# A selective scan between two ternary FFNs: a ring of five states in place of four, and the product with C written over the state

## The reference, cut to what matters

```python
skip = resid_norm @ W_skip                      # D=512 -> E=1024
x = _silu(conv(resid_norm @ W_in) + conv_b)     # 4 taps
delta = softplus(x @ W_delta_1 @ W_delta_2 + b_delta_2)
Bm, Cm = x @ W_B, x @ W_C                       # N=16 states
...
def step(h, inp):
    A_bar = jnp.exp(d_l[:, :, None] * A)
    h = h * A_bar + (d_l * x_l)[:, :, None] * B_l[:, None, :]
    y_l = jnp.einsum('ben,bn->be', h, C_l)
...
y_skip = (y + x * W_D) * _silu(skip)
return resid + y_skip @ W_out
```

## Time and profile before

| what | value |
|---|---|
| three runs, us | 2936.71, 2939.00, 2941.12; median 2939.0 |
| the profiled execution | 2940.29 us, its span 2938.7 |
| mean granted clock of PE | 0.97 |
| busy, share of the span | PE 90%, DVE 86%, POOL 82%, ACT 65% |
| chain that ended last | PE 61%, POOL 12%, DVE 8%, ACT 5%, issue 5%, DMA 3% |

### The profile page before, as it was taken

The page is one execution under the profiler, slowest core; times in us unless marked ns, Lnnn a source line. Parts: engine busy times, 40 slices in busy tenths (PEclk is TensorE's granted clock), DMA queues, the critical chain, the costliest instruction groups (busy, mean ns, idle before and its releaser), DMA issues.

```text
span 2938.7 us, 51656 instructions
## 1 busy us (share of the span) xinstructions
PE 2657.0 (90%) x17527; PEld 2054.0 (70%) x17527; DVE 2534.3 (86%) x3233; ACT 1900.3 (65%) x4428; POOL 2412.7 (82%) x2179
## 2 busy tenths in 40 slices
PE   4776899999999999999999999999999999999778
PEld 4555677776867777686777768677777867777555
DVE  6377899898889999898988989899998989899892
ACT  6375767666676766667676666767666676766651
POOL 1178888888898898989888898998989898897991
PEclk9888899999999999999999999999999999999898
DMA  7022222222222212222222131222213222221320
GB/s 261 31 60 69 62 53 69 49 53 72 51 70 53 70 46 55 73 51 69 53 65 50 48 80 44 71 58 64 51 49 79 48 69 57 65 51 48 87 55 15
DMA packets 91260, 185.22 MB, mean 63 GB/s; under 512 B 12220, under 2 KB 30456, under 8 KB 90488
## 3 DMA queue, kind: packets, MB, share of 16 engines
q1 hardware_dynamic: 72280, 113.76, 12.1%
q0 software_dynamic: 18720, 68.17, 11.8%
HBM read 104.82 MB, written 8.91 MB: 39 GB/s over the span
## 4 chain that ended last, share of the span: by engine, by line
PE 61%; POOL 12%; DVE 8%; ACT 5%; issue 5%; DMA 3%; POOLq 0%; DVEq 0%; ACTq 0%
PE ps L1560 20%; PE ps L1571 14%; PE ps L1583 10%; PE ps L1522 8%; POOL h L743 6%; PE ps L1632 5%; DVE h L1294 4%; DMA xw<-hc 3%; POOL hc L757 2%; PE ps L1593 2%; ACT ps L990 2%; DVE xc L1367 1%; POOL u L850 1%; POOL hl L842 1%; PE ps L1613 1%
## 5 line engine op out<-in xcount | busy, mean ns | idle before, releaser
L743 POOL TENSOR_TENSOR h<-u,bb 128x1024 f32<-128x1024 f32 x512 | 1247.1, 2436 | 82.5 <-PE ps L1522 36.7
L990 ACT ACTIVATE ps<-delta,a_neg 128x255 f32<-128x255 f32 x2048 | 877.0, 470 | 537.8 <-DVE h L1294 536.3
L1294 DVE TENSOR_TENSOR_SCAN h<-ps,h 128x512 f32<-128x512 f32 x1024 | 1189.5, 1203 | 27.3 <-ACT ps L990 13.2
L1560 PE MATMUL ps<-xh,q_up 128*128 128x256 f16 x2048 | 466.7, 275 | 38.0 <-DVE xl L1233 29.7
L1560 PE MATMUL ps<-xh,q_gate 128*128 128x256 f16 x2048 | 466.1, 274 | 28.4 <-DVE xw L1400 28.4
L1323 DVE SCALAR_TENSOR_TENSOR y<-ps,ccur,y 128x512 f32<-128x512 f32 x700 | 487.6, 737 | 1.7 <-PE ps L1522 1.1
L1522 PE MATMUL ps<-ident,h 128*128 128x128 f32 x3056 | 413.7, 278 | 64.0 <-DVE y L1323 58.8
L1560 PE MATMUL ps<-xl,q_up 128*128 128x256 f16 x2048 | 466.6, 275 | 0.0
L1560 PE MATMUL ps<-xl,q_gate 128*128 128x256 f16 x2048 | 465.5, 274 | 0.0
L1522 PEld LDWEIGHTS ps<-ident,h 128*128 128x128 f32 x3056 | 353.8, 142 | 135.4 <-issue 59.0
L842 POOL TENSOR_TENSOR hl<-act,hh 128x512 f16<-128x512 f32 x256 | 314.1, 1231 | 148.7 <-ACT hh L1015 148.7
(11 more groups left out here) (137 smaller groups left out, 3827.5 us busy)
## 6 DMA issues: line engine op xcount, KB each, us to landing
xw<-hc POOLq DMA_DIRECT2D x130, 512.0 KB, 4.5
bb<-b_scratch SPq DMA_DIRECT2D x224, 256.0 KB, 3.1
cplane<-c_scratch SPq DMA_DIRECT2D x130, 128.0 KB, 3.1
xs<-in_L_attn_resid_dram SPq DMA_DIRECT2D x17, 512.0 KB, 3.7
out_dram<-xs SPq DMA_DIRECT2D x16, 512.0 KB, 4.2
wraw<-in_L_ffn_W_up_dram SPq DMA_DIRECT2D x4, 1024.0 KB, 9.6
wraw<-in_L_ffn_W_gate_dram SPq DMA_DIRECT2D x4, 1024.0 KB, 12.5
wraw<-in_L_ffn_W_down_dram SPq DMA_DIRECT2D x4, 1024.0 KB, 14.1
```

The source lines that it names most:

```text
L743: pl.tensor_tensor(h[:, s % RING, :, :], u[:, :, :], bb[:, planes_of(s) % 2, s % PLANES:s % PLANES + 1, :].broadcast_to([P, HE, CH]), ALU. ...
L990: ins = ac.activation(abar[r][:, e, 1:], delta[:, k, 1:], ACT.Exp, scale=a_neg[:, k, n:n + 1])
L1294: v.tensor_tensor_scan(hr, abar[r].rearrange("p e t -> p (e t)"), hr, 0.0, ALU.mult, ALU.add).then_inc(scanned, 1)
L1560: ins = te.matmul(pp[:, f * CH:(f + 1) * CH], w[:, d, col:col + P], part[:, d, :], start=(d == 0 and part is xh), stop=(d == DB - 1 and pa ...
```

## The change

The ring has five slots, numbered by the running step (S % 5) in place of s % 4; `hc` is gone, so the memory is the same. The product with C is written over the state in its slot. It therefore waits for `carry_saved` of its own state, and the transfer reads the slot. The wait for the transfer before moves from ahead of the product to between product and transfer. A slot that held a product is free when its transfer has landed (`elem_added`), no more when the product is done. Every `u_times_b` waits for its planes of B, where before only the first of a pair did. `hidden_low` waits for the one before it. Three lists would move work from POOL to DVE (`UB_ON_DVE`, `Z_ON_DVE`, `LOW_ON_DVE`); they are empty, so the code for it issues nothing, and SP gets a second semaphore entry ahead of a load.

```diff
-RING = 4
+RING = 5
 ACTS = 2
+UB_ON_DVE = []
+Z_ON_DVE = []
+LOW_ON_DVE = {1: [], 2: []}
...
-        hc = sb("hc", [P, HE, CH])
...
-                    sp.wait_ge(ub_ready, STEPS * (c - (q < 2)) + last + 1)
+                    need(sp, ub_ready, ub_before(c - (q < 2), last + 1, False))
+                    sp.sem_inc(sp_go, 1)
+                    need(sp, dve_ub_ready, ub_before(c - (q < 2), last + 1, True))
                     sp.sem_inc(sp_go, 1)
...
-                if s == 0 or q > planes_of(s - 1):
-                    need(pool, bb_loaded[q % 2], 16 * planes_loaded(i, q))
...
+                if s in UB_ON_DVE:
+                    return
+                need(pool, bb_loaded[q % 2], 16 * planes_loaded(i, q))
                 used = S - RING
...
                 elif S >= RING:
-                    need(pool, times_c, elems_before(used // STEPS, used % STEPS) + 1)
+                    need(pool, elem_added, 16 * (elems_before(used // STEPS, used % STEPS) + 1))
...
                 need(pool, scanned, 2 * S + 2)
+                need(pool, carry_saved, S + 1)
+                go()
+                hs = h[:, S % RING, :, :]
+                pl.tensor_tensor(hs, hs, cplane[:, k:k + 1, :].broadcast_to([P, HE, CH]), ALU.mult).then_inc(times_c, 1)
+                need(pool, xw_ready, 2 * i + half + 1)
                 need(pool, elem_added, 16 * g)
-                go()
-                pl.tensor_tensor(hc[:, :, :], h[:, s % RING, :, :], cplane[:, k:k + 1, :].broadcast_to([P, HE, CH]),
-                                 ALU.mult).then_inc(times_c, 1)
-                need(pool, xw_ready, 2 * i + half + 1)
                 need(pool, times_c, g + 1)
-                pool.dma_start(xw[:, half * HE:(half + 1) * HE, :], hc[:, :, :], accum_op=ALU.add).then_inc(elem_added, 16)
+                pool.dma_start(xw[:, half * HE:(half + 1) * HE, :], hs, accum_op=ALU.add).then_inc(elem_added, 16)
...
                 need(pool, hh_ready, g + 1)
+                need(pool, hl_ready, g)
```

More of the change, by code:

```diff
@@ L317, in elems_before, with ub_before @@
     return sum(whole) + sum(k < s for k in elem_of(c))
+def ub_before(c, s, on_dve):
+    mine = [k for k in range(STEPS) if (k in UB_ON_DVE) == on_dve]
+    return len(mine) * c + sum(k < s for k in mine)
 def rows_before(c, s):
@@ L884, in run @@
                     for q in range(QT):
-                        if after(ph, f"YT_{q}", 0, s):
+                        if after(ph, f"YT_{q}", 0, s) and q not in Z_ON_DVE:
                             gated(ph, i, q)
                     for kind, p in hidden_units(ph, s):
-                        hidden_low(ph, i, kind, p)
+                        if p not in LOW_ON_DVE[kind]:
+                            hidden_low(ph, i, kind, p)
                     if after(ph, "DN1_1", 0, s):
@@ L995, in save_carry @@
                 need(sc, scanned, 2 * (STEPS * i + s + 1))
-                ac.activation(carry[:, s // N, :, state_of(s)], h[:, s % RING, :, CH - 1], ACT.Copy).then_inc(carry_saved, 1)
+                ac.activation(carry[:, s // N, :, state_of(s)], h[:, (STEPS * i + s) % RING, :, CH - 1], ACT.Copy).then_inc(carry_saved, 1)
             def first_decay(c, half):
@@ L1285, in _, with u_times_b @@
             ve.wait_ge(scale_step, 12)
+            def u_times_b(i, s):
+                S, half, n = STEPS * i + s, s // N, state_of(s)
+                q, g = planes_of(s), ub_before(i, s, True)
+                need(ve, bb_loaded[q % 2], 16 * planes_loaded(i, q))
+                need(ve, u_ready, 2 * i + half + 1)
+                need(ve, x0_ready, 2 * i + half + 1)
+                used = S - RING
+                if S >= RING and not is_elem(used // STEPS, used % STEPS):
+                    need(ve, hT_ready, 2 * rows_before(used // STEPS, used % STEPS) + 2)
+                elif S >= RING:
+                    need(ve, elem_added, 16 * (elems_before(used // STEPS, used % STEPS) + 1))
+                need(ve, carry_saved, used + 1)
+                go()
+                v.tensor_tensor(h[:, (STEPS * i + s) % RING, :, :], u[:, :, :],
+                                bb[:, q % 2, s % PLANES:s % PLANES + 1, :].broadcast_to([P, HE, CH]),
+                                ALU.mult).then_inc(dve_ub_step, 1)
+                need(ve, dve_ub_step, g + 1)
+                v.tensor_tensor(h[:, (STEPS * i + s) % RING, :, 0], h[:, (STEPS * i + s) % RING, :, 0], a0[:, half, :, n], ALU.add).then_inc(dve_ub_ready, 1)
             def scan_of(i, s):
                 S = STEPS * i + s
-                need(ve, ub_ready, S + 1)
+                if s in UB_ON_DVE:
+                    need(ve, dve_ub_ready, ub_before(i, s + 1, True))
+                else:
+                    need(ve, ub_ready, ub_before(i, s + 1, False))
                 for r in range(2):
                     need(ve, abar_ready, 2 * S + r + 1)
-                    hr = h[:, s % RING, 2 * r:2 * r + 2, :].rearrange("p e t -> p (e t)")
+                    hr = h[:, (STEPS * i + s) % RING, 2 * r:2 * r + 2, :].rearrange("p e t -> p (e t)")
                     v.tensor_tensor_scan(hr, abar[r].rearrange("p e t -> p (e t)"), hr, 0.0, ALU.mult, ALU.add).then_inc(scanned, 1)
@@ L1401, in y_plus_x, with hidden_low @@
                 ins.then_inc(bank_used[bk], 1)
+                if q in Z_ON_DVE:
+                    need(ve, bank_used[bk], job_no(ph, i, f"YT_{q}")[1] + 1)
+                    go()
+                    v.tensor_tensor(gz[:, qb, :], yx, gz[:, qb, :], ALU.mult).then_inc(z_ready, 1)
+            def hidden_low(ph, i, kind, p):
+                need(ve, hh_ready, PAIRS * ffn_run(ph, i, kind) + p + 1)
+                need(ve, hl_ready, PAIRS * ffn_run(ph, i, kind) + p)
+                v.tensor_tensor(hl[:, 2 * p:2 * p + 2, :], act[:, p % ACTS, :].rearrange("q (f t) -> q f t", f=2),
+                                hh[:, 2 * p:2 * p + 2, :], ALU.subtract).then_inc(hl_ready, 1)
             def run(ph, i):
@@ L1412, in run @@
                         scan_of(*step)
+                    for kind, p in hidden_units(ph, s - 1):
+                        if p in LOW_ON_DVE[kind]:
+                            hidden_low(ph, i, kind, p)
                     if s == MASK_H and "IN_0" in PHASES[ph]:
@@ L1429, in run @@
                         ternary(2, 4 + r, r * F, F)
+                    step = step_of(ph, i, s + U_AHEAD)
+                    if step and step[1] in UB_ON_DVE:
+                        u_times_b(*step)
                     for name in results(ph, s, late=True):
```

19 lines of the change are left out of this document (11 added, 8 removed).

## The result

The changed kernel takes **2952.5 us** (median of 7 runs, 2949.7 to 2954.7) against 2939.0 us before (7 runs, 2936.6 to 2944.0): a ratio of 1.004, 95% interval 1.003 to 1.0051. It is 0.3 to 0.5% slower. The profiled execution took 2954.6 us with a span of 2952.8, 14.1 more than the span before.

What follows compares the result with a forecast made beforehand. PE was taken as the bound, tied to POOL by one chain in each half chunk. 0.83 us over 14 middle chunks gave 11.6, plus 1.5 and 1 at the ends: 14.1 us, so 2953 us, range 2946 to 2960.

Steps and rivals of the forecast that it cites:

- What bounds the kernel: Middle chunks: PE is the bound, idle 8.2 us each; two chains, one per half, tie it to POOL through DVE.
- Step 10's 1.38 us: First half: POOL's wait for PE's transposes goes with five slots, so step 10 starts 1.38 us earlier per chunk.
- the entries: Extra POOL queue entries: +0.045 us per affected u*B, +0.125 per `hidden_low` pair; 0.43 in the second half.
- The landing before step 13: First half: step 13 waits for state 8's transfer, landing in 5.1 us, and starts 0.43 us later than before.
- The first rival: Transfers land within 3.4 us, so step 13 waits for nothing and the kernel takes 2926 us; chance 0.10.
- The rest of the first half: After step 13: -0.13 at step 14, +0.04 at step 15, +0.09 at steps 16 and 17; half about 0.4 us later.
- The second half: To state 31's issue: two `hidden_low` pairs (+0.25) and four u*B (+0.18) make it 0.43 us later per chunk.
- the pieces at steps 24 and 25: POOL's waits for transposes there lie ahead of its wait for `hh`; removing them was counted as nothing.
- The ends: Last chunk +1.5 us from landings, removed waits and queue entries; first chunk 0 to 3, taken as 1.
- Faster: Same as the first rival: landings within 3.4 us let POOL keep about 1.25 us per chunk; 2926 us, chance 0.10.
- No change: Entries hidden everywhere, or state 8's transfer lands in 4.5 us: each about 2943, both 2935; chance 0.24.
- Much slower: State 8's transfer takes 7.2 us to land in a third of the chunks, 10 us more: 2963; chance 0.08.

Runs made afterwards that it cites:

- e5: Changed kernel without the two added waits (planes at every step, `hidden_low` for its predecessor) and with state 9 multiplied on POOL for state 8: 2936.7 us, ratio 0.9979.
- e10: Changed kernel without the two added waits and with state 7 multiplied on POOL in place of state 8: 2934.4 us, ratio 0.9986.
- e1: Kernel before plus only the added waits (planes at every u*B, `hidden_low` for its predecessor), ring of four and `hc` kept: 2953.6 us, ratio 1.0038.
- e7: Changed kernel without only the wait of `hidden_low` for its predecessor; the planes' wait at every step stays: 2952.0 us, ratio 1.0036.
- e4: Changed kernel, added waits kept, with state 9 multiplied on POOL in place of state 8 in the middle chunks: 2943.1 us, ratio 1.0007.
- e2: Changed kernel (ring of five, product in place) without the two added waits: 2947.6 us, ratio 1.0019.
- e6: Kernel before with state 9 multiplied on POOL in place of state 8: 2956.8 us, ratio 1.0054.
- e8: e5 with other states multiplied on POOL in the last chunk (3, 6, 7, 12, 15, 21, 27, 30): 2937.4 us, ratio 0.9982.

## Why the prediction was right, and where it was right by luck

The time, 2953 forecast and 2952.5 measured, is right, and so is the mean chunk: 0.83 forecast, 0.79 measured. The spans even agree to the tenth, 14.1 us each, but from 11.6 + 1.5 + 1 forecast and 11.0 + 2.9 + 0.2 measured. By steps:

- **What bounds the kernel:** held. PE's busy time didn't move, and its waits for DVE grew at the two named places (28.4 to 36.3 and 33.9 to 39.2 us, 0.56 and 0.38 a chunk where 0.4 each was forecast). DVE's own wait rose to 69.0, forecast 73.
- **Step 10's 1.38 us:** held. From the issue of state 31 to step 10 the mean went from 37.57 to 36.25, 1.33 less (1.40 by the medians); 1.29 was forecast with the entries. The gap is gone in all 14 middle chunks.
- **The landing before step 13:** held nearly to the number. From the issue of state 31 to step 13 the mean went from 50.93 to 51.38: +0.45, forecast +0.43 (by the medians +0.62). The landing took 5.1 us on the mean, the value taken from the row of that transfer. By the fixed 2.0 us and 436 GB/s that the Trainium skill gives ("DMA: Bandwidth & Descriptors", section "Anatomy of one DMA - SWDGE (gpsimd) path") it would be an estimated 3.2 us; the shortest of the 130 after the change took 4.5, so the measurement decides against it. The first rival, which needed such a landing, forecast 2926; with the early landing out of the way and without the waits the kernel takes 2934 to 2937 (e5, e10).
- **The rest of the first half: mis-sized.** Forecast +0.4 to the issue of state 15's transfer, measured +0.71 (+0.81 by the medians). The missing 0.31 is the step that isn't in the prediction at all: the issue itself, 0.86 us behind its product in place of 0.55. The entries were costed as gaps between u*B's; that one more of them can come with a later issue wasn't in any row of before. By e1 and e7 it comes with the wait in `hidden_low`; how, is open.
- **The second half: right terms, one missing.** The entries were forecast at +0.43; e1 has +0.34, e4 less e5 +0.39, changed less e2 +0.66 (by the medians 0.33, 0.41 and 0.41). The pair of `hidden_low` grew by 0.18 to 0.19, not 0.125: its second starts 0.14 us behind the end of the first and not 0.07 to 0.08. But the half as a whole came out at +0.07, because of what the sum held at nothing: "POOL only gets there earlier and waits longer" for the pieces at steps 24 and 25. In e2 the second half is 0.59 shorter than before (0.33 by the medians). POOL's wait for `hh` did grow, from 6.6 to 7.0 us a middle chunk, so a part is lost as said; the rest is not. From PE's start behind its first stall to POOL's last pair of `hidden_low` the median is 44.5 to 44.7 us in the three kernels with a ring of four and `hc` (before, e1, e6) and 44.0 to 44.3 in the seven with a ring of five, so the gain comes with the ring and lies between those two points. POOL starts step 24 earlier against the issue of state 15 by 0.8 us a chunk (0.45 by the medians), its u*B's can reach DVE's scans and PE's transposes sooner, and `hh` is itself behind PE. That last link is argued from the order and not shown by a run.
- **So two errors cancel:** +0.31 left out in the first half, -0.36 in the second. The sum was nearer than its parts.
- **The ends:** the last chunk cost 2.9, forecast 1.5; the ramp and chunk 0 cost 0.2, forecast 1, though four landings hold POOL up there for 4.7 us, where two were expected. In the last, steps 11 and 13 lost 1.07 and 1.08 (forecast 1.1 each) and step 28 1.08 (forecast 0.87 + 0.2). Left out were step 15 with 0.54, for the landing of state 10, which takes 5.1 and not the median 4.5, and step 4 with 1.07, for that of state 31 of the chunk before; by step 6 there is 0.6 of it left, since POOL waits less for DVE in between.
- **Rivals.** Faster: only if the landing is short, and it isn't. No change: neither of its conditions came true, the entries show and state 8 still lands in 5.1. Much slower: the longest landing was 6.4 and not where it counts. The wait for `carry_saved` cost nothing that shows, as forecast; only e8 brought it out, with 2.12 us before its last product. Two figures of the rivals were off: with the 2.5 us of the ends in the sum, the change would turn to a gain at a landing of 4.1, not 4.3, and each half of "no change" gives 2944 to 2945, not 2943.
- **The cause in one line:** what makes the kernel slower is the added waits and the slots held until a landing, above all that of state 8, and not the fifth slot. Without the added waits it is level per chunk and 0.1 to 0.3% slower in all; with another state chosen for POOL as well (7 or 9 for 8) it is 0.05 to 0.3% faster than before.

## What to carry to other kernels

When a buffer is given up by working in place, its slot is then held until the transfer out of it has *landed*: list for each slot the other work of the issuing engine between the issue and the step that wants the slot, against that transfer's own landing, and move the few that don't fit before judging the change; here, with the added waits gone, one number in the list of eight states decided between slower and faster. A deeper ring and an order of work tuned for the shallower one belong together, and the change of the one should be measured with the other re-chosen. And waits that always find their semaphore ready weren't free on POOL, which runs densely here (e1: 0.2 to 0.5%); ask for what is already known once, not at each step.

## What the runs showed of the hardware that was not expected

- The issue of a transfer on POOL can start 0.29 us later than its neighbours of the same kind, and further waits in the queue can bring that on at one place in every chunk: state 15's issue stands 0.83 to 0.88 us behind its product's end in e1, e4 and the changed kernel, with the further wait in `hidden_low`, and 0.55 to 0.58 in every kernel without it. Why is open: the issues of states 3 and 22, with the same wait right behind them, kept 0.57 (0.55 in e1), and one or two issues elsewhere are as late in most kernels without it.
- An instruction of POOL that waits for its own predecessor's end started 0.14 us after that end (the pair of `hidden_low`: 2.46 us), while without the wait the second starts 0.04 us before the first has ended (2.27 us). So such a wait costs 0.19 us a pair, in all 28 pairs of a kernel.
- The landing of the 512 KB accumulating transfer depends on when in the chunk it is issued: 5.1 to 5.2 us on the mean for those of state 8 or 9, issued 60 to 66 us after the chunk's start, 4.6 for that of state 7, issued at 56, and 4.5 to 4.6 for that of state 11, issued at 77 to 85. Which of the other transfers makes the difference no run tells.
